# Grouped attention stage of a fused block: four score banks, three other banks, and an earlier order of stacks and maxima

## What is computed

```python
q = x @ Wq.T ; k = x @ Wk.T ; v = x @ Wv.T        # 32 query heads, 8 key/value heads of width 8
scores = einsum('bsqhd,bthd->bqhst', qh, kh) * scale
probs = softmax(scores, axis=-1)
a_dot = einsum('bqhst,bthd->bsqhd', probs, vh)
sigma_q = elu(q) ; a_mem = sigma_q @ memory / (sigma_q @ memory_norm)
out = a_dot * (1.0 - w) + a_mem * w
```

## Time and profile before

| what | value |
|---|---|
| profiled execution | 4549.46 us (span from first to last instruction 4547.7) |
| median of three runs | 4559.63 us |
| TensorE, VectorE, ScalarE busy over the span | 84%, 57%, 37% |
| mean granted TensorE clock over the span | 0.915 |
| the 31 steady groups of the grouped stage | 3346 to 3971 us, 625 us |

### The profile page before, as it was taken

How to read it: one execution, slowest core, us unless ns; L and a number is a source line. 1 busy time by engine, 2 the same in 40 slices (tenths; PEclk the granted TensorE clock), 3 DMA queues, 4 the chain that set the end, 5 groups by cost and what they waited for, 6 DMA issues and landing times.

```text
span 4547.7 us, 45570 instructions
## 1 busy us (share of the span) xinstructions
PE 3830.8 (84%) x16352; PEld 2483.2 (55%) x16352; DVE 2576.8 (57%) x4355; ACT 1675.3 (37%) x2871; POOL 1356.0 (30%) x1074
## 2 busy tenths in 40 slices
PE   6869778887978874898999887999878888879999
PEld 4647534435844432555555546788644444457887
DVE  5645356664456652768677755433356666654333
ACT  2433246653235540232323233222245555532222
POOL 3234312214320102333323314444221211143442
PEclk8979889998989996999999998999989999989999
DMA  1010000001000002100010111000000000010000
GB/s 56 1 38 5 29 1 1 1 1 42 1 22 5 5 10 78 26 19 25 18 26 17 26 31 41 21 29 5 16 1 1 1 1 1 1 58 21 26 12 19
DMA packets 32765, 83.35 MB, mean 18 GB/s; under 512 B 6304, under 2 KB 7456, under 8 KB 32288
## 3 DMA queue, kind: packets, MB, share of 16 engines
q1 hardware_dynamic: 32544, 80.44, 5.7%
HBM read 59.44 MB, written 4.19 MB: 14 GB/s over the span
## 4 chain that ended last, share of the span: by engine, by line
PE 53%; DVE 23%; ACT 5%; POOL 3%; issue 2%; DMA 1%; SPq 0%; DVEq 0%; POOLq 0%; ACTq 0%
PE ps L226 11%; PE ps L228 10%; PE ps L227 10%; DVE max_cols L1149 7%; PE ps L1096 4%; DVE max_cols L2142 3%; PE ps L1090 2%; PE ps L296 2%; PE ps L1081 2%; DVE q_lo L2126 2%; ACT probs L1126 1%; PE ps L1086 1%; PE ps L800 1%; PE ps L1940 1%; PE ps L1077 1%
## 5 line engine op out<-in xcount | busy, mean ns | idle before, releaser
L1149 DVE TENSOR_REDUCE max_cols<-ps 128x1 fp32r<-128x512 f32 x1024 | 635.9, 680 | 285.6 <-PE ps L1081 284.9
L1126 ACT ACTIVATE probs<-ps 128x512 f32<-128x512 f32 x1024 | 546.4, 603 | 247.0 <-PE ps L1090 157.0
L754 POOL TENSOR_TENSOR h_lo<-h,h_hi 128x512 fp32r<-128x512 f32 x304 | 392.5, 1291 | 815.3 <-ACT h_hi L834 815.3
L911 DVE TENSOR_TENSOR gated<-silu,ps 128x512 f32<-128x512 f32 x288 | 198.0, 688 | 687.2 <-PE ps L228 657.4
L828 ACT ACTIVATE silu<-ps 128x512 f32<-128x512 f32 x304 | 181.9, 598 | 926.8 <-PE ps L228 926.7
L226 PE MATMUL ps<-xn_hi,w_hi 128*128 128x512 f32 x1216 | 479.4, 394 | 0.0
L227 PE MATMUL ps<-xn_lo,w_hi 128*128 128x512 f32 x1216 | 476.0, 391 | 0.0
L228 PE MATMUL ps<-xn_hi,w_lo 128*128 128x512 f32 x1216 | 475.6, 391 | 0.0
L330 POOL CAST o_hi<-o_scaled 128x512 fp32r<-128x512 f32 x64 | 39.1, 612 | 897.2 <-DVE o_scaled L1171 897.2
L1096 PE MATMUL ps<-probs,v_aug 128*32 128x512 f32 x2048 | 302.1, 665 | 0.0
L226 PEld LDWEIGHTS ps<-xn_hi,w_hi 128*128 128x128 f32 x1216 | 230.7, 190 | 49.4 <-issue 1.0
(11 more groups left out here) (463 smaller groups left out, 7899.0 us busy)
## 6 DMA issues: line engine op xcount, KB each, us to landing
raw<-in_w_ffn SPq DMA_DIRECT2D x76, 448.0 KB, 3.3
raw<-raw SPq DMA_DIRECT2D x256, 64.0 KB, 2.0
composed_inputs<-in_m_latent SPq DMA_DIRECT2D x1, 5120.0 KB, 15.6
raw<-in_w_mamba SPq DMA_DIRECT2D x8, 448.0 KB, 6.0
raw<-in_w_latent SPq DMA_DIRECT2D x5, 448.0 KB, 16.9
x<-in_x SPq DMA_DIRECT2D x4, 512.0 KB, 6.5
gated_pattern<-gated SPq DMA_DIRECT2D x4, 512.0 KB, 3.1
raw<-gated_pattern SPq DMA_DIRECT2D x4, 512.0 KB, 4.2
```

Of the source, the lines that this page charges most:

```text
L754: nc.gpsimd.tensor_tensor(HL[:, b % 3, :], hb[:, b % 2, :], HH[:, b % 3, :].bitcast(F32), ALU.subtract).then_inc(G.sem, G.step((s, ev)))
L911: nc.vector.tensor_tensor(ga if routed(i) else hb[:, i % 2, :], sg[:, i % 2, :], bank[2 + i % 2], ALU.mult).then_inc(V.sem, V.step((s, "ga ...
L1126: nc.scalar.activation(self.PB[:, n % 8, :], self.scores(n), ACT.Exp, scale=self.scale).then_inc(A.sem, A.step((s, ("exp", n))))
L1149: nc.vector.tensor_reduce(self.MB[:, self.tile_of(g, h) % 2, q, col:col + 1], self.psum(ev), op=ALU.max, axis=AX.X, negate=True).then_inc( ...
```

## The change

For the grouped stage alone (`k_tiles` not 0): four banks for scores and three for the rest (before three and four); three buffers for `q_stack` and not two; the stack of g+2 (and at j = 6 the keys of the next batch) at slot 8 and not 11; and the 16 maxima in the slots of U0 to U2, where they were spread over all four units. The bias stays at slot 10. `rotary` and `pattern` keep all their values.

```diff
-        AUXB = (3, 4, 5, 7)
-        SCORES = (0, 1, 2)
+                self.SCORES, self.AUXB, self.NQ = ((0, 1, 2, 3), (4, 5, 7), 3) if k_tiles else ((0, 1, 2), (3, 4, 5, 7), 2)
-                self.QS = alloc("q_stack", [P, 2, self.tiles, L], F32R)
+                self.QS = alloc("q_stack", [P, self.NQ, self.tiles, L], F32R)
...
-                        for pos, count in ((0, 1), (1, 3), (3, 3), (4, 2), (6, 2), (7, 2), (9, 3)):
+                        early, late = ((0, 2), (1, 2), (3, 4), (4, 2), (6, 4), (7, 2)), ((0, 1), (1, 3), (3, 3), (4, 2), (6, 2), (7, 2), (9, 3))
+                        for pos, count in early if self.k_tiles else late:
                             self.slots[g][pos] = mx[had:had + count] + self.slots[g][pos]
                             had += count
...
-                        self.slots[g][11] = self.stacks(g + 2) + self.slots[g][11]
+                        made = 8 if self.k_tiles else 11
+                        self.slots[g][made] = self.stacks(g + 2) + self.slots[g][made]
```

More of the change, by code:

```diff
@@ L985, in q_rows @@
                 r = slice((h % self.per) * self.rows, (h % self.per + 1) * self.rows)
-                return self.QS[:, g % 2, h // self.per, :] if self.k_tiles else self.QS[r, g % 2, h // self.per, :]
+                return self.QS[:, g % self.NQ, h // self.per, :] if self.k_tiles else self.QS[r, g % self.NQ, h // self.per, :]
             def k_tile_no(self, g, h):
@@ L1025, in psum @@
             def psum(self, ev):
-                return bank[AUXB[self.aux_no[ev] % len(AUXB)]]
+                return bank[self.AUXB[self.aux_no[ev] % len(self.AUXB)]]
             def step_no(self, g, kt, h):
@@ L1031, in scores @@
             def scores(self, n):
-                return bank[SCORES[n % len(SCORES)]]
+                return bank[self.SCORES[n % len(self.SCORES)]]
             def free(self, s, ev, by_act, by_vec):
-                if ev[0] in self.reader and self.aux_no[ev] >= len(AUXB):
-                    old = self.order[self.aux_no[ev] - len(AUXB)]
+                if ev[0] in self.reader and self.aux_no[ev] >= len(self.AUXB):
+                    old = self.order[self.aux_no[ev] - len(self.AUXB)]
                     (by_act if self.reader[old[0]] is A else by_vec).append((s, old))
@@ L1058, in pe @@
                         by_vec.append((s, ("bias", g, h // self.per)))
-                    if n >= len(SCORES):
-                        by_act.append((s, ("exp", n - len(SCORES))))
+                    if n >= len(self.SCORES):
+                        by_act.append((s, ("exp", n - len(self.SCORES))))
                 elif kind == "pv":
@@ L1114, in act @@
                     act.wait_ge(PE.sem, PE.at((s, ev)))
-                    nc.scalar.activation(self.QS[:, g % 2, t, :], self.psum(ev), ACT.Copy).then_inc(A.sem, A.step((s, ev)))
+                    nc.scalar.activation(self.QS[:, g % self.NQ, t, :], self.psum(ev), ACT.Copy).then_inc(A.sem, A.step((s, ev)))
                 elif kind == "v":
@@ L1152, in vec @@
                     g, t = ev[1:]
-                    q = self.QS[:, g % 2, t, :]
+                    q = self.QS[:, g % self.NQ, t, :]
                     dve.wait_ge(PE.sem, PE.at((s, ev)))
```

## The result

The changed kernel took 4518.50 us as the median of six runs (4513.58 to 4536.55), against 4560.89 for six runs of the kernel before: ratio 0.992, interval 0.9904 to 0.9935. By that ratio it is 36 us (29 to 44) or 0.8% less, and 42 us by the two medians, against 53 by the sum of the prediction. The profiled execution has a span of 4526.6 us, 21 less than before. It reached the grouped stage 11 us later than the execution before had, took 3 us more for the stage's start and 34 us less for its steady part. So the comparison by stage says more than that of the spans.

The account below looks back on a forecast made before the run. The prediction took the grouped stage as bound by the order of the engines' waits, no engine being full. Three batches (47 us) and the last (6) gain 53: 4549.5 to 4496.5, plus half of 10, gives 4502 us; range 4472 to 4545.

Parts of the forecast that it names:

- The fourth score bank at the tanh: At j = 3 and 6, the fourth score and a pv go ahead of the wait: 4.0 us gained each (1 to 5.7).
- the walk: Event-by-event timing of a group in the new order: 15.4 us plain, 18.0 us with projection and tanh.
- The keys' stacks: At j = 7, TensorE has more work to run while the stacks block ScalarE: 2.0 us gained (0 to 3).
- The plain group: A group without side work takes 15.4 us where it took 15.83: 0.4 us gained.
- The projection and the front: At j = 4 and 0, matmuls cost 1.85 us, not VectorE's 3.33: 1.6 us gained; `xn` at j = 0 adds 0.5.
- `xn` stands in a gap: At j = 0, `xn` lies in a gap between the last maximum and the bias: 0.5 us more gained.
- The start of the stage: Its 16 maxima in a row are bound by VectorE with three banks as with four: no change.
- The last batch: Gains 6 us: eight times 0.4 and two projections.
- The clock's rival: TensorE's longer hollow behind the norm brings low clock in all 31 groups, 25 us lost: 4527 us; chance 0.17.
- Three banks starve VectorE: In the grouped stage, three other banks starve VectorE or the low clock stays: slower, 4569 us; chance 0.08.

Follow-up runs that it names:

- the old banks and both moves: Changed kernel with norm at slot 9, tanh activations at slot 5, and three score and four other banks again: 4481.68 us against 4556.84 for the kernel before.

## Why the prediction came out as it did

The direction was right, the measured time lies in the range, and the gain came where the stage has its long waits; but only two thirds of the forecast gain came. The terms for the two long waits held; those for the plain group, the projection, the front and the start of the stage did not: the window over the 31 groups, which the prediction put near 572 us, is 594. (Its chances for a time below 4537 add up to 0.86 and not 0.84, which changes nothing.) By its own steps:

- **The fourth score bank at the tanh**: forecast 4.0 a group, measured 4.0 and 3.1 in the table (3.2 and 2.4, 6.3 and 2.8 in the other batches; 3.6 on average), to a group of 18.40 at j = 3 where the walk gave 18.0. j = 6 takes 20.65, as its bias waits 1.05 us for the bank of the first key stack. The mechanism is shown from two sides: with three score banks the wait is 3.36 again, and with the tanh moved in the old kernel the groups shrink by themselves. What the prediction did not say is how little each part is worth alone. In the second and third batch j = 3 takes 21.2 to 21.3 with the banks alone, 21.5 in the new order with the old banks, 20.8 with the old maxima, and 19.15 with the late stacks, against 18.4: at the tanh it takes the bank and the early maxima. Over the steady part (627.75 before, 594.03 after) it is 618.86 with the banks alone, 619.47 without them, 619.79 without the early stacks and 605.14 without the early maxima: most of the gain needs the banks and the early stacks together.
- **The keys' stacks**: forecast 2.0, measured 0.8, 3.9 and 2.1 in the three batches (3.3, 3.9 and 2.2 with the changed kernel's second trace). So the size was right on average. How much low clock would go was a guess, and it is what makes the batches differ: the changed kernel's group is the longer the lower its clock (24.68 us at 0.79, 23.74 at 0.86, 22.14 at 0.92). The bias waits 1.05 us for the first key stack's bank, where the prediction had 2.8.
- **The plain group**: forecast 15.4, measured 15.96, so 0.1 lost where 0.4 was expected. The order of events was as walked: the hollow stands before the fourteenth product (1.67 us beyond the free spacing, where the walk had 1.9; the trace lists 1.50, as it counts from the end of the matmul before), the wait for the stack's copy is gone, VectorE idles 0.44 (measured 0.56) before the fifth. What was missing are the changes between kinds of matmul. The walk counted 0.23 before each pv and behind the first matmul after it; the trace has 0.32 from a free product to the pv, 0.41 from the last held product to the pv (3561.63 to 3562.04), and 0.33 from the first matmul after a pv to the next, which stood in rows 5 already (3546.98 to 3547.31). Around the pv behind U0's scores they bring the fifth maximum 0.3 later than walked (3.81 and not 3.5 after the first score), and through the norm most of the delay of the last product follows (11.58 and not 11.2). Before the pv behind the last product they bring 0.2 more. The pv between disappears in the hollow, and the bias took 0.48 where 0.6 was counted. That gives 15.96 where the walk's own sum is 15.5, of which the prediction took 15.4. Over 31 groups the 0.56 is 17 us, as the walks with side work start from this one.
- **The projection and the front**: forecast 2.0 at j = 4 and 2.5 at j = 0, measured on average 0.1 and 0.0 over three batches, and j = 1 lost 1.1. The price of the old place was taken from the worst case. VectorE's 3.33 us came with a low clock just before (0.73 from 3596 to 3600); at full clock, in the next batch, it idled 1.78 us there, which is no more than the 1.85 that the eight matmuls add to the tail:

```profile
3768.06 0.75 DVE L2395 SCALAR_TENSOR_TENSOR x<-ps,mix,x 128x512 f32<-128x512 f32 x1 [1.78 <-PE ps L2299]
```

  (Also, 3.33 less 1.85 is 1.5 and not 1.6.) In the last batch, with the projection as the only side work and at full clock, it cost 2.6 us before (18.45 against 15.84) and costs 1.9 now (17.83 against 15.97): 0.7 gained. "`xn` stands in a gap" failed too: VectorE's queue is in order, and `xn` stands behind `out`, which TensorE delivers at the end of its tail. The next rows show the changed kernel's VectorE there, and TensorE's first score of j = 1:

```profile
3684.91 0.75 DVE L2396 SCALAR_TENSOR_TENSOR x<-ps,mix,x 128x512 f32<-128x512 f32 x1 [2.38 <-PE ps L2300]
...
3686.60 1.29 DVE L324 TENSOR_TENSOR xc<-xc,dev 128x512 f32<-128x512 f32 x2
3687.81 0.68 DVE L1156 TENSOR_TENSOR q_stack<-q_stack,ps 128x512 fp32r<-128x512 f32 x1
```

```profile
3688.64 0.47 PE L1091 MATMUL ps<-q_stack,k_alone 128*128 128x512 f32 x1 [1.45 <-DVE q_stack L1156]
```

The bias is late by `xn`, and the score, with all behind it, waits 1.45 us (0.60 in the kernel before).

- **The start of the stage** was put at nothing. From the clearing of `k_alone` to the first bias it is 49.8 us before and 52.9 after. It varies over the traces, and the shortest two had the highest clock (0.70, the others 0.56 to 0.63). Four traces with the old banks have 49.8 to 51.6, ten with the new 51.5 to 52.9: the means differ by 1.7 us. Whether that comes from the banks, and by which event, was not tried.
- **The last batch** came near its forecast (5.1 for 6) by luck: the prediction had 0.4 in every plain group there, but the plain groups at full clock lost 0.1, and most of the gain came from low stretches of the clock, of which the changed kernel's trace has fewer.
- **The clock's rival** did not come about. Its price was right: a plain group with a low stretch behind the hollow takes 17.55, 1.6 more. But it is rare. The last batch has five groups without side work, which took 15.84, 17.30, 17.53, 15.82 and 17.01 before and take 15.97, 15.98, 17.55, 16.01 and 15.52 now: three with a low clock became one. The stage's clock rose. The traces show that the longest waits, at the tanh and the keys, got shorter; that this is what raised the clock was not isolated. Nor is the clock by itself the gain: with the banks changed alone it is 0.97 as well, and the steady part still takes 618.86 us, while with the tanh moved alone it is 0.95 and the steady part takes 601.21. What the prediction drew from the Trainium skill ("TensorE: Matmul & The Clock Gate", section "A second HAM failure mode: psum-queue depth-cycling"), that fewer rotating banks are a loss by the clock, did not decide here: with one rotating bank less the clock was higher, 0.97 against 0.93, also with the banks changed alone; and with the old banks and both moves it is 0.97 too.
- **Three banks starve VectorE** was given too little: it did not turn the sign, but it is a real cost. The banks alone made plain groups 0.8 longer, and with the norm and the tanh out of the way the fourth other bank is worth 0.6 in each plain group and 13 to 18 us in all.

## What to carry to other kernels

When an in-order engine stands behind a wait, first move the wait: three activations put a unit later gave more than half of what a bank, a buffer and a new order gave together (23 us, 12 to 34, against 36, 29 to 44). Banks that are taken from one rotation for another have a price per round that has to be set against the rare wait they cover, and the balance turns when that wait is gone. Three spreads of the maxima moved idle time from one gap to another; what shortened the loop was to put work (the norm) into the gap that was left. And a wait read in one window isn't the price of a place: look at the same place in the other rounds, at full clock, before it goes into a sum (1.78 us here, and not 3.33).

The version with the norm at slot 9, ScalarE's tanh at slot 5, early stacks and maxima and the old banks takes 4481.68 us, 75 less than the kernel before and 44 less than the changed kernel on the same chip. Whether it still needs the early maxima, the early stacks and the third query buffer was not tried.

## What the runs showed of the hardware

A held matmul costs more than the wait that the trace lists. In the changed kernel's plain group, 512-column matmuls that run freely start 0.23 us apart. The fourteenth product starts 1.90 us after the thirteenth (3558.54 to 3560.44), 1.67 more than that, while the listed wait is 1.50: it counts from the end of the matmul before. The products that follow are handed a bank by VectorE one at a time and start 0.59 to 0.60 us apart (3560.44, 3561.04, 3561.63), which is the pace of VectorE's maxima (3.64 us for six). The pv starts 0.41 us behind the last of them, where it starts 0.31 to 0.32 behind a matmul that was not held. Every earlier stage of the kernel is the same, yet the grouped stage (the clearing of `k_alone`) began between 3277.1 and 3297.5 us in the fourteen traces; so the spans of two single executions that differ by less than some 20 us don't tell two kernels apart.
